# A chunk of ten tiles instead of twelve: nine gathers by GpSimd and one pick by TensorE, in twelve rounds of a ring of 26

## The reference

```python
h = jnp.maximum(_layernorm(x, axis=-1), 0.0)
x_i, x_j = h[dst], h[src]
feat = jnp.concatenate([x_i, x_j - x_i], axis=-1)
m = jnp.maximum(feat @ W1 + b1, 0.0) @ W2 + b2
out = jax.ops.segment_max(m, dst, num_segments=12500)
return x + jnp.where(jnp.isneginf(out), 0.0, out)
```

## Time and profile before

| | us |
|---|---|
| median of 3 runs | 5022.33 (5005.23 to 5023.61) |
| the profiled execution | 5046.15, its span 5044.3 |
| PE, DVE, ACT, POOL busy | 3240.3, 2493.6, 1025.4, 3109.6 |
| loop with gathers, first to last start of a round | 738 to 4627 |
| last 26 chunks without gathers | to 4889 |
| end | to 5044 |

### The profile page before, as it was taken

The page is one execution under the profiler, slowest core; times in us unless marked ns, Lnnn a source line. Parts: engine busy times, 40 slices in busy tenths (PEclk is TensorE's granted clock), DMA queues, the critical chain, the costliest instruction groups (busy, mean ns, idle before and its releaser), DMA issues.

```text
span 5044.3 us, 58734 instructions
## 1 busy us (share of the span) xinstructions
PE 3240.3 (64%) x14598; PEld 1876.2 (37%) x14861; DVE 2493.6 (49%) x8363; ACT 1025.4 (20%) x4057; POOL 3109.6 (62%) x3186
## 2 busy tenths in 40 slices
PE   2100137777777777777777777777777777777970
PEld 2100014444444444444444444444444444444540
DVE  4100115555555555555555555555555555556871
ACT  4300212212122121221212222122221212212320
POOL 5777756666666666666666666666666666664017
PEclk8555558888888888888888888888888888888985
DMA  7866312222222222222222222222222222222222
GB/s 274 315 229 227 115 32 73 67 73 70 70 73 67 73 70 70 70 70 73 70 70 69 70 73 69 70 70 69 73 67 73 70 70 72 69 72 71 80 77 56
DMA packets 239614, 452.86 MB, mean 90 GB/s; under 512 B 94781, under 2 KB 95402, under 8 KB 238738
## 3 DMA queue, kind: packets, MB, share of 16 engines
q1 hardware_dynamic: 97663, 225.75, 14.2%
q0 software_dynamic: 103216, 117.29, 11.1%
q10 hardware_dynamic: 38362, 105.62, 5.4%
HBM read 230.84 MB, written 217.71 MB: 89 GB/s over the span
## 4 chain that ended last, share of the span: by engine, by line
another core or an unknown queue 41%; issue 28%; DVE 10%; ACT 9%; PE 7%; POOL 2%; ACTq 2%; DMA 1%; DVEq 1%; POOLq 0%; SPq 0%
ACT dst_all L549 5%; DVE state L911 4%; PE ps_g L676 4%; DVE a_fill L885 3%; PE ps_m L696 2%; POOL a_rows L456 2%; ACT zt L560 2%; ACTq L567 1%; DMA shared<-in_x_dram 1%; DVE rows L897 1%; ACT zt L474 1%; ACT keep L531 1%; PE ps_t L687 0%; ACT shared L501 0%
## 5 line engine op out<-in xcount | busy, mean ns | idle before, releaser
L393 POOL DMA_INDIRECT rows<-b_table,src_idx x2865 | 2785.5, 972 | 1523.6 <-issue 805.7
L676 PE MATMUL ps_g<-shared,dst_all 128*128 128x512 bf16 x9468 | 2318.6, 400 | 174.3 <-issue 170.5
L676 PEld LDWEIGHTS ps_g<-shared,dst_all 128*128 128x128 bf16 x9731 | 1011.1, 105 | 1329.5 <-issue 417.3
L696 PE MATMUL ps_m<-w_diag,zt 128*128 128x128 f32 x3126 | 707.8, 411 | 920.2 <-ACT zt L560 917.8
L696 PEld LDWEIGHTS ps_m<-w_diag,zt 128*128 128x128 f32 x3126 | 638.2, 308 | 1056.3 <-ACT zt L560 1049.8
L911 DVE SCALAR_TENSOR_TENSOR state<-state,keep,ps_m 128x64 f32<-128x64 f32 x3125 | 862.3, 276 | 202.5 <-PE ps_m L696 166.7
L885 DVE SCALAR_TENSOR_TENSOR a_fill<-a_fill,keep 128x64 f32<-128x64 f32 x3144 | 879.6, 280 | 53.1 <-DVE a_fill L885 41.6
L935 DVE TENSOR_TENSOR dst_all<-ps_s,page_keys 128x1664 bf16<-128x1664 f32 x132 | 249.6, 1891 | 816.0 <-remote 795.1
L935 DVE TENSOR_TENSOR dst_all<-ps_x,page_keys 128x1664 bf16<-128x1664 f32 x132 | 249.6, 1891 | 794.7 <-remote 774.7
L560 ACT ACTIVATE zt<-ps_t 128x512 f32<-128x512 f32 (+1 forms) x521 | 226.4, 486 | 1517.9 <-remote 1511.6
L549 ACT ACTIVATE dst_all<-ps_g,dst_all 128x64 f32<-128x64 f32 x2096 | 458.1, 347 | 33.2 <-DVE rows L944 33.2
(11 more groups left out here) (116 smaller groups left out, 877.0 us busy)
## 6 DMA issues: line engine op xcount, KB each, us to landing
a_edges<-state SPq DMA_DIRECT2D x80, 1250.0 KB
a_fill<-a_edges SPq DMA_DIRECT2D x260, 384.0 KB
states<-state ACTq DMA_DIRECT2D x260, 384.0 KB
rows<-b_table,src_idx POOLq DMA_INDIRECT x2865
src_idx<-in_src_dram SPq DMA_DIRECT2D x234, 6.0 KB
shared<-in_x_dram SPq DMA_DIRECT2D x5, 625.0 KB
b_table<-shared ACTq DMA_DIRECT2D x5, 625.0 KB
a_table<-a_rows SPq DMA_DIRECT2D x1, 3125.0 KB
```

Of the source, the lines that this page charges most:

```text
L393: nc.gpsimd.indirect_dma_start(out=rows[:, slot, t * C:(t + 1) * C], out_offset=None, in_=b_table, in_offset=at(src_idx[:, slot, :], t)).t ...
L676: last = nc.tensor.matmul(ps_g[:, half, :], key_is[:, half, g, :], table[:, g, t, :], start=(g, t) == (0, 0), stop=g == PAGES - 1)
L696: last = nc.tensor.matmul(ps_m[:, g, a * C:(a + m) * C], zt[0:m * C, g, a * C:a * C + P], w2_pair[0:m * C, 0:m * C], start=True, stop=True)
```

## The change

One number changes, and all that is derived from it.

```diff
-    CHUNK = 12
+    CHUNK = 10
     RING = 26
     ITERS = TILES // (CHUNK * RING)
```

## The result

| | before | after | ratio (95% interval) |
|---|---|---|---|
| median of 4 runs each | 5019.24 us (5005.23 to 5023.61) | 5093.30 us (5088.26 to 5105.30) | 1.0156 (1.0127 to 1.0185) |
| the profiled execution, its span | 5046.15, 5044.3 | 5088.96, 5087.1 | |
| mean granted TensorE clock | 0.794 | 0.836 | |

The change makes the kernel **1.6% slower** in these runs: inside the range (4985 to 5140), but 61 us above the likeliest forecast (5032). So the two spans differ by 42.8 us and the medians by 74. How the loop of before divided in those four runs is not known, since none of them was profiled.

What follows compares the result with a forecast made beforehand. Something behind GpSimd was taken to serve gathers at 1.40 us each, holding TensorE's releases. Loop +63.5, ahead of it -45, last chunks -9 sum to +9.5 us: 5032 us forecast against 5022.33, range 4985 to 5140.

Steps and rivals of the forecast that it cites:

- rival 1: Loop: gathers count 1.25 us and the remaining wait is fixed; 14.12 us a round, 5133 us; chance 0.18.
- (a): Loop: two gathers fewer a round at 1.40 us each, 286 rounds of 13.82 us instead of 234: +63.5 us.
- (b): Loop: other engines' added work lies beside the gathers; TensorE needs 11.9 of 13.82 us, idle stretch about one microsecond.
- Rival 2: Loop: TensorE becomes the bound; at 15 us a round +347 us, or 5369 us; chance 0.07.
- (c): Ahead of the loop: 52 transfers fewer, but scatters wait for SP's zeros: -45 us, between -30 and -73.
- (d): Last 26 chunks: each loses a transpose and a pair of W2 matmuls: -9 us.
- Rival 3: Loop: releases no longer come late, GpSimd alone bounds; 12.4 us a round, 4626 us; chance 0.07.

Runs made afterwards that it cites:

- h1: The changed kernel, unedited, run again in a later session: 5050.97 us, 1.0012 of the kernel before.
- h2: Kernel before with 33 instead of 21 pick matmuls between the transposes and the wait for the relu: 5157.53 us, ratio 1.0228.
- g1: Kernel before with nine instead of eleven gathers in each loop round, all other twelve-tile work kept: 4393.39 us.
- g2: Changed kernel with seven instead of nine gathers in each loop round, all other ten-tile work kept: 4262.28 us.
- sessions 1 and 2: Two follow-up sessions in which the unedited kernel before took 4076.36 and 4075.49 us.

## Why the prediction was right, and where it was wrong

**What bounds the loop: right.** Something takes the gathers at a steady pace slower than GpSimd's 1.25 us, and TensorE's releases wait for it. The wait behind the burst stays when gathers go, and rounds shrink by more than 1.25 a gather. The prediction took 1.40; the runs give 1.38 to 1.42. The forecast round of 13.82 stands against 13.77 in h1 and a median of 13.66 in the measured profile. What the something is stays open.

**The time: inside the range in part by luck.** 5093 lies above the forecast's own range (4990 to 5070). It is covered only because the range was drawn wide enough for rival 1, and rival 1 is refuted.

**(a) The loop: right in the ordinary round, wrong in taking all 286 as ordinary.** The 220 rounds outside pairs took 13.69 us in the mean. With that throughout the loop would be 3915 us; it was 3989.6, 74 more, which is what the pairs cost. The step that failed is that one length of round was multiplied by 286. Against the forecast loop of 3952.5 the ordinary rounds gave 37 us back and the pairs took 74. An estimate from this: without pairs the changed kernel's median would be 5093 - 74 = 5019, that of before, as in h1. In before all rounds were alike, and this was read as a property of the mechanism. The rounds of after and h2 say that it hung on the place of the transposes as well: in before they come at 6.7 us and later, where a short round is rare (3 in 327).

**(b) The cover on TensorE: the sentence that hid it.** Rival 2 argued that "shorter idle stretches leave the clock up rather than down", which is right (0.83 to 0.89 in the loop), and used it only against TensorE as a bound. But a TensorE that is done sooner can transpose earlier in the burst: in after the median is 6.7 us instead of 7.5 behind its first gather, and 12 rounds have it before 4.5. This was not followed up. That TensorE bounds nothing is right: ahead of the W2 products it was idle 418 us in after, 1.3 a chunk, near the one microsecond forecast (920 before, show one of 3.35); in h1, without pairs, 2.2 a chunk.

**(c) Ahead of the loop: -51.3 instead of -45, in h1 697.87 - 738.35 = -40.5.** The mechanism was right: the zeros, just hidden before, are waited for, 38 us. They landed earlier than forecast (508.81 against 520), since SyncE was back at its early pace from about 495 and not 502.

**(d) The last chunks: right.** 9.70 us a chunk, -6.5 instead of -9 (-11.0 in h1).

**The sum.** Without pairs it can be read off h1, whose session's before (5045.33) is near the profile that the prediction used: -40.5 + 48.4 - 11.0 = -3.1 us of span, where +9.5 was forecast, and a measured ratio of 1.0012. In the session of the result it is -51.3 + 100.6 - 6.5 = +42.8.

**The rivals.** Rival 1 (1.25 and a fixed wait, 14.12 a round) falls with g1 and g2; its 5133 would have been nearer to the 5093 measured than 5032, but for a reason that is not there. Rival 2 is refuted. Rival 3 (releases no longer late, GpSimd alone the bound) came true in two ways that its price, 4626, does not cover. In sessions 1 and 2 it holds for before as well, with 1.25 a gather and no 1.1 us beside them: 11.36 a round after the change. In the measured session it holds in 33 single rounds (11.53), and each is more than paid back by the next. The argument against it, that five short gathers prove nothing for nine, was right on average and missed that single releases could slip through.

## What to carry to other kernels

Where a loop's rounds are all alike, ask what keeps them so before multiplying one of them; a wait that looks like waste (here 2 to 3 us behind each burst) can be what keeps two bursts from running into one. When an engine gets faster or its idle time shorter, work out which release it now gives sooner and what that triggers, not only whether the engine still has cover. And compare only within a session: this change was 1.3% faster, 0.1% and 1.6% slower beside the same kernel before, while the time of that kernel moved from 4076 to 5047 us.

## What the runs showed of the hardware that was not expected

- The kernel before took 4076.36 us in one session and 5047.04 in another on the same chip, each within 0.25%. In the first indirect transfers go out every 1.25 us and no engine waits for a late release; in the second 1.4 us are the pace, and `z_turned` reaches ACT some seven microseconds late. The granted clock of before differs too (0.87 and 0.795). The cause was not found; the transfers' packets take the same time in both. The Trainium skill, NOTIFIC — the notification-queue block, section 7.1 on overflow, says that a queue of event records whose ring is full stalls the engine that writes to it in one of its three modes, and in the other two drops or overwrites records. No run here shows whether that is what holds TensorE; it was not tried.
- While 18 gathers follow one another without a pause, TensorE runs one pick in 1.4 to 2.8 us (741.73, 744.53 above) although the program has it wait for nothing between them, and the release of products that ended at 739.20 is seen at 753.80, 14.6 us late. That the late release behind nine or eleven gathers is the same thing in small is likely, but not shown.
- In the slower sessions the pace is one of the number of indirect transfers (all of one size here), not of the other transfers or the other work of a chunk: twelve tiles with nine gathers and ten tiles with nine gathers both take 13.8 us.
